# One tile of a 78-stage row sort is sorted by place and its four words are fetched through GpSimd

## The chip, the cores and the metric

The kernel runs on one core of one Trainium2 chip. Its time is device microseconds (us) for one execution, 17144.38 us in the median of three runs. VectorE is called DVE, ScalarE ACT, TensorE PE, GpSimd POOL and SyncE SP, as the profile does.

## What is computed

The input x is 32 images of 32 channels of 56x56 float32. Four layers follow each other, each as `x = x + layer(groupnorm(x))`. The last one holds nearly all the time:

```
xs = sort(x[:, :16], over rows), then sort over columns        # idx_h, idx_w kept
q  = conv1x1(x); qkv = fused 3x3/5x5/7x7 depthwise convs of q  # q1, k1, q2, k2, v
idx = argsort(v, over the 3136 pixels of a channel)
out1 = attention(q1[idx], k1[idx], v[idx]); out2 = attention(q2[idx], k2[idx], v[idx])
out = conv1x1(unsort(out1) * unsort(out2)); then both image sorts are undone on 16 channels
```

So each of the 1024 rows (batch, channel) of 3136 pixels is sorted by v, and four further words of each pixel (q1, k1, q2, k2) have to end in the same order.

## The kernel before

The rows lie as T = 8 tiles of 128 partitions; tile t holds batches 4t to 4t+3. All working buffers are slices of one SBUF tensor `arena`; `masks` holds four byte masks. Each engine has its own instruction list, and the work goes in rounds: at the end of a round every engine reports (`end_round`, L240) and SP opens the next one when all four have (`close_round`, L246). The rounds after the first layers:

- Four rounds **b** (`b_sync`, `b_scalar`, `b_vector`, L801 to L893) sort the images by rows and columns. U = 4 groups of eight batches, in the order 0, 1, 2, 3. From the second on, `c` of tile 0 runs beside them.
- **c** (`c_sync`, `c_tensor`, `c_scalar`, L923 to L975) makes the five words of one tile: SP loads 7 chunks of the padded image in 16 DMAs each (L930), PE makes 5 groups per chunk of 112 matmuls each (L951), so 35 groups, and ACT moves each from PSUM into `pay[b]` (four words, interleaved) or `vrow[b]` (L967). It makes a tile for the next round.
- Eight rounds **d** (`d_sync`, `d_scalar`, `d_vector`, L990 to L1098), here called d0 to d7, sort one tile each. The sorting network has 78 stages (`ROW_NET`). In a stage ACT first keeps the lower partners (of v at L1010, of the four words at L1020, in two lots). DVE compares v (L1046, a byte mask), takes minimum and maximum (L1054, L1061), and with the mask copies the upper partners down (L1070) and the kept ones up (L1077), each element four words wide. SP stores each mask to HBM (`row_masks`, L994), since the sort is undone later.
- **e** (`e_sync`, `e_scalar`, `e_vector`, `e_tensor`, L1146 to L1337) is the attention of a sorted tile. It ends with a store of the product (`prodd`, L1150).
- Two rounds **u** undo the row sort of four tiles each, with the masks loaded again; `u_first_sync` and `u_first_scalar` (L1437 to L1452) load and interleave the first four products. Two rounds **g** undo the image sorts.

What runs beside a sort is a Python generator: after each stage the sort calls `next(beside, None)` SLOTS = 4 times on SP, ACT and DVE, so a stage has four slots and a round 312. `c` evicts one group per four slots, the first after eight slots. `e` ends at slot 160 (E_LAST + 4). In round d(t), e of tile t-1 and c of tile t+1 run beside the sort:

```
d_sync(sp, 0, c_sync(sp, 1, CHUNKS, SLOTS))
...
d_sync(sp, i * 2 + k, chain(e_sync(sp, i * 2 + (k - 1)), c_sync(sp, i * 2 + (k + 1), CHUNKS, SLOTS)))
...
d_sync(sp, T - 1, chain(e_sync(sp, T - 2), u_first_sync(sp)))
u_sync(sp, 0, e_sync(sp, T - 1))
```

POOL has no work in the program: it takes part in the round ends only.

Of the kernel before, what the change touches and what calls it, by code (L numbers as in the profile page):

```python
# [16 lines left out]
N = H * W  # L17
P = 128
# [164 lines left out]
def program(nc, x, wdct_t, keep, ident_in, same_batch, same_head, shifts, sw, gate_w, temp,  # L183
# [4 lines left out]
    with ctx:  # L188
# [6 lines left out]
        rd = nc.dram_tensor("rd", (B * C, N), f32).ap()  # L195
        row_masks = nc.dram_tensor("row_masks", (T, P, ROW_PAIRS), u8).ap()
# [33 lines left out]
        sems = {}  # L230

        def sem(name):
            if name not in sems:
                sems[name] = ctx.enter_context(nc.semaphore(name))
            return sems[name]
# [10 lines left out]
        def close_round(sp, used):  # L246

            sp.wait_ge(round_done, len(go))
            for s in used:
                sp.sem_clear(s)  # L250
            sp.sem_clear(round_done)
            for n in go:
                sp.sem_inc(go[n], 1)  # L253
# [10 lines left out]
        s_const, s_rows, s_imgw, s_img, s_ydct = (sem(n) for n in (  # L264
            "s_const", "s_rows", "s_imgw", "s_img", "s_ydct"))
        s_chain, s_sq_in, s_sq_out = sem("s_chain"), sem("s_sq_in"), sem("s_sq_out")
        s_dct1, s_dct1c, s_dct2, s_dct2c = (sem(n) for n in ("s_dct1", "s_dct1c", "s_dct2", "s_dct2c"))
        s_taps, s_wmm, s_wcp = sem("s_taps"), sem("s_wmm"), sem("s_wcp")
        s_zero, s_norm = sem("s_zero"), sem("s_norm")
# [167 lines left out]
        a_x, a_y, a_st3, a_stp = sem("a_x"), sem("a_y"), sem("a_st3"), sem("a_stp")  # L437
        a_ch, a_sqi, a_sqo, a_norm = sem("a_ch"), sem("a_sqi"), sem("a_sqo"), sem("a_norm")
        a_sq, a_n2, a_n2e, a_nrm, a_nt = sem("a_sq"), sem("a_n2"), sem("a_n2e"), sem("a_nrm"), sem("a_nt")
        a_wide, a_rt, a_rni, a_sp = sem("a_wide"), sem("a_rt"), sem("a_rni"), sem("a_sp")  # L440
        a_g0, a_q, a_pr, a_dot, a_s, a_g, a_acc, a_half = (sem(n) for n in (
            "a_g0", "a_q", "a_pr", "a_dot", "a_s", "a_g", "a_acc", "a_half"))
        a_yv, a_yc, a_e, a_x3, a_xp = sem("a_yv"), sem("a_yc"), sem("a_e"), sem("a_x3"), sem("a_xp")
# [333 lines left out]

        b_in, b_out, b_mst = sem("b_in"), sem("b_out"), [sem(f"b_mst{i}") for i in range(4)]
# [17 lines left out]
        def b_begin(sp):  # L796

            b_load(sp, 0, bin_, b_in)
            b_load(sp, 0, bx, b_out)

        def b_sync(sp, u, beside, more=True):  # L801
            count = [0] * 4
            for d in range(2):
                for s, (at, _, n) in enumerate(IMG_NET):
# [8 lines left out]
                    if q == 5 and more:  # L813
                        sp.wait_ge(b_cp, 1)
                        sp.sem_clear(b_in)
                        b_load(sp, u + 1, bin_, b_in)
# [8 lines left out]
            if not more:  # L825
                sp.wait_ge(b_out, 16 * UB)
# [131 lines left out]
        def c_scalar(act, b, chunks, pace):  # L958

            n = 0  # L960
            for _ in range(2 * pace):
                yield
            for r in chunks:
# [138 lines left out]

        E_ROOT, E_RECIP, E_SCALE, E_TR, E_SEG, E_SEGS, E_OUT, E_NEXT = 8, 14, 16, 24, 8, 40, 76, 68
# [3 lines left out]
        e_sems = list(es.values())  # L1107
        st = [WS_AT]
# [37 lines left out]
        def e_sync(sp, t):  # L1146
            pace = Pace()
            yield from pace.to(E_LAST)
            sp.wait_ge(es["oc"], 16)
            sp.dma_start(prod_t[t], eo).then_inc(es["st"], 16)  # L1150
            sp.wait_ge(es["st"], 16)

        def e_scalar(act, b):
            e, pace = es, Pace()
# [78 lines left out]
        def e_vector(dve, b):  # L1233
            e, pace = es, Pace()
# [41 lines left out]
        def e_tensor(pe, b):  # L1276
            e = es
# [150 lines left out]
        prod_t4 = prodd.rearrange("(r w p) n -> r w p n", w=NP, p=P)  # L1428
        x3_t4 = x3d.rearrange("(r w p) n -> r w p n", w=NP, p=P)
        row_masks_t4 = row_masks.rearrange("(r w) p n -> r w p n", w=NP)  # L1430
        rd_t4 = rd.rearrange("(r w b c) n -> r w b c n", w=NP, b=TB, c=C)
        out_t4 = out.rearrange("(r w b c) n -> r w b c n", w=NP, b=TB, c=C)
# [4 lines left out]
        def u_first_sync(sp):  # L1437
# [3 lines left out]
            for w in range(NP):  # L1441
                if w >= 2:
                    yield from pace.to(8 + 12 * w)
                    sp.wait_ge(u_in, w - 1)
                sp.dma_start(uws[w % 2], prod_t4[0, w]).then_inc(u_ld[w], 16)
# [8 lines left out]
        def u_sync(sp, r, beside):  # L1454
            for i in range(SR):
# [3 lines left out]
                for w in range(NP):  # L1459
                    sp.dma_start(masks[:, w, 0:n], row_masks_t4[r, w, :, at:at + n]).then_inc(u_raw, 16)  # L1460
                for _ in range(SLOTS):
                    next(beside, None)
                if i == 60:
                    for _ in beside:
                        pass
                    for w in range(3):
                        sp.dma_start(u_x3[w], x3_t4[r, w]).then_inc(u_x[w], 16)
                    if r == 0:
                        for w in range(NP):
                            sp.dma_start(u_late[w], prod_t4[1, w]).then_inc(u_ld[w], 16)  # L1470
                    else:
                        g_load(sp, 0)
            for w in range(NP):
                sp.wait_ge(u_ev, 7 * (w + 1))
                for b in range(TB):
                    sp.dma_start(rd_t4[r, w, b, 0:CS], u_pr[w % 2][C * b:C * b + CS, :]).then_inc(u_rst[w % 2], 16)
                sp.wait_ge(u_add, 7 * (w + 1))
                for b in range(TB):
                    sp.dma_start(out_t4[r, w, b, CS:C], u_x3[w % 3][C * b + CS:C * b + C, :]).then_inc(u_ost, 16)
                if w == 0:  # L1480
                    sp.wait_ge(u_ost, 16 * TB)
                    sp.dma_start(u_x3[0], x3_t4[r, 3]).then_inc(u_x[0], 16)
# [170 lines left out]
        C_FIRST = [(0, 1, 2), (3, 4), (5, 6)]  # L1653

        @block.sync
        def _(sp):
# [15 lines left out]
            b_sync(sp, 0, iter(()))  # L1672
            close_round(sp, b_sems)
            for u in range(1, U):
                b_sync(sp, u, c_sync(sp, 0, C_FIRST[u - 1], 1), more=(u < U - 1))
                close_round(sp, b_sems + c_sems)
            d_sync(sp, 0, c_sync(sp, 1, CHUNKS, SLOTS))
            close_round(sp, d_sems + c_sems)
            with sp.Fori(0, (T - 2) // 2) as i:
                for k in (1, 2):  # L1680
                    d_sync(sp, i * 2 + k, chain(e_sync(sp, i * 2 + (k - 1)), c_sync(sp, i * 2 + (k + 1), CHUNKS, SLOTS)))
                    close_round(sp, d_sems + e_sems + c_sems)
            d_sync(sp, T - 1, chain(e_sync(sp, T - 2), u_first_sync(sp)))
            close_round(sp, d_sems + e_sems + u_first_sems)
            u_sync(sp, 0, e_sync(sp, T - 1))
# [11 lines left out]
        def _(pool):  # L1697
# [9 lines left out]
            with pool.Fori(0, U + T):  # L1707
                end_round(pool, "pool")
            end_round(pool, "pool")
# [5 lines left out]
        def _(act):  # L1715
# [14 lines left out]
            for u in range(1, U):  # L1730
                b_scalar(act, c_scalar(act, 0, C_FIRST[u - 1], 1))
                end_round(act, "act")
            d_scalar(act, 0, c_scalar(act, 1, CHUNKS, SLOTS))
            end_round(act, "act")
            with act.Fori(0, (T - 2) // 2):
                for k in (1, 0):
                    d_scalar(act, k, chain(e_scalar(act, 1 - k), c_scalar(act, 1 - k, CHUNKS, SLOTS)))
                    end_round(act, "act")
            d_scalar(act, 1, chain(e_scalar(act, 0), u_first_scalar(act)))
# [10 lines left out]
        def _(dve):  # L1750
# [18 lines left out]
            d_vector(dve, 0, iter(()))  # L1769
            end_round(dve, "dve")  # L1770
            with dve.Fori(0, (T - 2) // 2):
                for k in (1, 0):
                    d_vector(dve, k, e_vector(dve, 1 - k))
                    end_round(dve, "dve")
            d_vector(dve, 1, e_vector(dve, 0))
# [10 lines left out]
        def _(pe):  # L1786
# [14 lines left out]
            for u in range(1, U):  # L1801
                c_tensor(pe, C_FIRST[u - 1])
                end_round(pe, "pe")
            c_tensor(pe, CHUNKS)
            end_round(pe, "pe")
            with pe.Fori(0, (T - 2) // 2):
                for k in (1, 0):
                    e_tensor(pe, 1 - k)
                    c_tensor(pe, CHUNKS)
                    end_round(pe, "pe")  # L1810
            e_tensor(pe, 0)
            end_round(pe, "pe")
# [50 lines left out]
```

## Time and profile before

| | |
|---|---|
| median of 3 runs | 17144.38 us (17140.89 to 17151.51) |
| the profiled execution's own time | 17148.49 us |
| its span, first to last instruction | 17146.6 us |
| DVE busy | 16016.6 us, 93% of the span |
| ACT busy | 7247.1 us, 42% |
| PE busy | 6760.6 us, 39% |
| POOL busy | 0.2 us |
| DMA packets | 297993, 509.96 MB, 10% of 16 engines |

The profile is one execution; its time stands 4 us over the median. The trace behind it can be asked for any stretch: instructions in order of time, groups by line, the busy time of each engine per stretch, and the DMAs with the time from issue to landing. "Idle before" is the time an engine stood still before an instruction, with what ended it behind the arrow.

### The profile page before, as it was taken

Reading aid. Unit: us, or ns where it says so; the run is one execution under the profiler, and the core shown is the slowest. Engines: PE = TensorE matmul, PEld = TensorE weight load, DVE = VectorE, ACT = ScalarE, POOL = GpSimd, SP = SyncE. Lnnn points to the kernel's source line nnn. Section 1 sums busy time; section 2 is a strip of 40 time slices with the busy share of each in tenths; the row PEclk is TensorE's granted clock in tenths of the full one; section 3 lists DMA queues with packets and bytes.
Section 4 is the critical chain, followed back from the end, with each engine's and each line's share of the span. In section 5 each row is a group of like instructions: output and inputs, shape, how many; then the busy total and the mean of one; then the engine's idle time right before and its main releaser. Section 6 shows DMA issues by size and latency. Waiting matters only on the chain.

```text
span 17146.6 us, 106420 instructions
## 1 busy us (share of the span) xinstructions
PE 6760.6 (39%) x40644; PEld 2812.9 (16%) x40644; DVE 16016.6 (93%) x10433; ACT 7247.1 (42%) x5055; POOL 0.2 (0%) x4
## 2 busy tenths in 40 slices
PE   6888855570025614613722632642561101210010
PEld 4444431120011111201211211211111000000000
DVE  6999988899999999999999999999999998879978
ACT  0000003343453453444444444345345337868854
POOL 0000000000000000000000000000000000000000
PEclk9999987785567757856866866875775555555555
DMA  0000012110001000000100100100100001131232
GB/s 18 13 25 17 21 37 71 54 31 11 10 10 31 23 10 26 27 10 22 31 10 10 40 15 10 35 19 10 31 23 10 25 14 41 52 86 51 71 73 65
DMA packets 297993, 509.96 MB, mean 30 GB/s; under 512 B 54685, under 2 KB 258685, under 8 KB 287413
## 3 DMA queue, kind: packets, MB, share of 16 engines
q1 hardware_dynamic: 297460, 502.90, 10.3%
q8 instruction: 330, 5.41, 0.1%
q14 instruction: 203, 1.65, 0.0%
HBM read 298.39 MB, written 204.33 MB: 29 GB/s over the span
## 4 chain that ended last, share of the span: by engine, by line
DVE 60%; issue 10%; ACT 6%; PE 3%; DMA 1%; SPq 1%; DVEq 0%; ACTq 0%
DVE arena L1070 21%; DVE arena L1077 15%; DVE arena L1054 5%; DVE masks L1046 5%; DVE arena L1061 5%; DVE arena L1550 3%; PE psum L1332 2%; ACT arena L1497 2%; DVE arena L1548 2%; ACT arena L1020 2%; DVE arena L1401 1%; ACT arena L1507 1%; DMA masks<-row_masks 1%; ACT arena L1010 1%; DVE arena L1407 1%
## 5 line engine op out<-in xcount | busy, mean ns | idle before, releaser
L1020 ACT ACTIVATE arena<-arena 128x4096 f32<-128x4096 f32 (+26 forms) x1456 | 3072.3, 2127 | 5883.2 <-DVE arena L1077 5883.0
L951 PE MATMUL psum<-arena,wt 128*32 128x448 f32 x31360 | 3379.9, 594 | 1873.0 <-ACT arena L967 1126.7
L1070 DVE COPY_PREDICATED arena<-masks,arena 128x4096 f32<-128x4096 uint8 (+26 forms) x1456 | 4017.3, 2787 | 9.3 <-ACT arena L1020 9.3
L1077 DVE COPY_PREDICATED arena<-masks,arena 128x4096 f32<-128x4096 uint8 (+26 forms) x1456 | 4001.3, 2775 | 0.6
L951 PEld LDWEIGHTS psum<-arena,wt 128*32 128x32 f32 x31360 | 1047.2, 119 | 4208.2 <-issue 2660.3
L1287 PE MATMUL psum<-ident,arena 128*112 128x128 f32 x896 | 194.4, 386 | 3557.8 <-ACT arena L1208 2826.6
L1550 DVE COPY_PREDICATED arena<-arena 128x2048 f32<-128x2048 uint8 (+28 forms) x364 | 972.2, 2687 | 241.8 <-ACT arena L1507 241.6
L1046 DVE TENSOR_TENSOR masks<-arena 128x1568 uint8<-128x1568 f32 (+21 forms) x912 | 1033.9, 1192 | 128.9 <-ACT arena L1010 128.9
L731 PE MATMUL psum<-arena 128*128 128x392 f32 x3072 | 1053.8, 496 | 31.9 <-DVE arena L633 31.8
L1054 DVE TENSOR_TENSOR arena<-arena 128x1568 f32<-128x1568 f32 (+21 forms) x912 | 1056.3, 1220 | 0.0
L1061 DVE TENSOR_TENSOR arena<-arena 128x1568 f32<-128x1568 f32 (+21 forms) x912 | 1037.6, 1197 | 0.3
L1497 ACT ACTIVATE arena<-masks 128x4704 uint8<-128x4704 uint8 (+20 forms) x156 | 966.6, 6196 | 102.7 <-DMA masks<-row_masks 102.6
L1548 DVE COPY_PREDICATED arena<-arena 128x2048 f32<-128x2048 uint8 (+28 forms) x364 | 972.6, 2687 | 10.0
L1010 ACT ACTIVATE arena<-arena 128x1568 f32<-128x1568 f32 (+21 forms) x912 | 881.0, 997 | 79.0 <-SPq L253 68.3
L1507 ACT ACTIVATE arena<-arena 128x2048 f32<-128x2048 f32 (+28 forms) x364 | 762.9, 2120 | 276.2 <-DVE arena L1548 276.0
L1332 PE MATMUL psum<-arena 128*128 128x392 f32 x1024 | 583.6, 742 | 497.3 <-ACT arena L1178 378.8
L705 PE MATMUL psum<-arena 128*128 128x448 f32 (+1 forms) x1536 | 674.8, 589 | 252.0 <-DVE arena L621 220.3
L1323 PE MATMUL psum<-ident,arena 128*128 128x128 f32 x256 | 71.4, 434 | 1749.2 <-DVE arena L1266 1749.2
L1287 PEld LDWEIGHTS psum<-ident,arena 128*112 128x112 f32 x896 | 151.6, 197 | 3620.9 <-ACT arena L1208 2838.6
L1580 PE MATMUL psum<-arena,projm 128*128 128x448 f32 x112 | 88.8, 968 | 1596.5 <-DVE arena L1548 1596.5
L731 PEld LDWEIGHTS psum<-arena 128*128 128x128 f32 x3072 | 577.7, 191 | 481.9 <-DVE arena L633 86.5
L1302 PE MATMUL psum<-arena 112*128 112x512 f32 x896 | 486.9, 707 | 0.0
(126 smaller groups left out, 6794.2 us busy)
## 6 DMA issues: line engine op xcount, KB each, us to landing
arena<-xpad SPq DMA_DIRECT2D x896, 108.5 KB, 2.4
xpad<-arena SPq DMA_DIRECT2D x8, 1924.0 KB, 7.0
arena<-in_x SPq DMA_DIRECT2D x8, 1568.0 KB, 10.4
x3d<-arena SPq DMA_DIRECT2D x8, 1568.0 KB, 5.2
prodd<-arena SPq DMA_DIRECT2D x8, 1568.0 KB, 5.2
arena<-prodd SPq DMA_DIRECT2D x8, 1568.0 KB, 13.8
arena<-x3d SPq DMA_DIRECT2D x8, 1568.0 KB, 10.1
out<-arena SPq DMA_DIRECT2D x64, 196.0 KB, 4.5
```

The source lines that it names most:

```text
L731: last = nc.tensor.matmul(psum[:, i, 0:392], diag[:, kk, :], gg[2 * (g % 2) + n][:, 392 * i:392 * i + 392], start=False, stop=(g % NH == N ...
L951: last = nc.tensor.matmul(psum[C * b:C * b + C, n % C_BANKS, 0:CROWS * W], wt[:, g, C * w:C * w + C], cx[i % 2][b][:, y0:y0 + CROWS, x0:x0 ...
L1010: last = nc.scalar.activation(packed_view(vtmp, at, piece, 1), pair_views(vrow[b], piece, 1)[0], ACT.Copy)
L1020: last = nc.scalar.activation(packed_view(ptmp, here, piece, NP), pair_views(pay[b], piece, NP)[0], ACT.Copy)
L1046: last = nc.vector.tensor_tensor(packed_view(masks[:, q % 4, :], at, piece, 1), packed_view(vtmp, at, piece, 1), pair_views(vrow[b], piece ...
L1054: last = nc.vector.tensor_tensor(lo, packed_view(vtmp, at, piece, 1), hi, ALU.min)
L1061: last = nc.vector.tensor_tensor(hi, packed_view(vtmp, at, piece, 1), hi, ALU.max)
L1070: last = nc.vector.copy_predicated(lo, wide_mask(q, piece, at), hi)
L1077: last = nc.vector.copy_predicated(hi, wide_mask(q, piece, at), packed_view(ptmp, here, piece, NP))
L1497: nc.scalar.activation(um[i % 3][:, 0:NP * n].rearrange("p (n w) -> p w n", w=NP), masks[:, :, 0:n], ACT.Copy).then_inc(u_mk, 1)
L1548: last = nc.vector.copy_predicated(hi, mask, packed_view(utmp, here, piece, NP))
L1550: last = nc.vector.copy_predicated(lo, mask, hi)
```

## The change

Tile 7 is now the first one sorted, in a round of its own called **s**, and its four words are not moved by the network.

- The b rounds go in the order 3, 0, 1, 2, and c of tile 7 runs beside the last three.
- In round s, POOL writes into `spos` the number of each element (`128 rows x 3136`). The network moves v and this one position word: per stage DVE has compare, minimum, maximum and two single-word predicated copies, and ACT two keeps. SP first stores the four words of the tile to HBM (`payd`, 6.4 MB, 401,408 records of 16 bytes). c of tile 0 runs beside it.
- Then seven rounds d0 to d6 sort tiles 0 to 6 as before. POOL is not waited for at their ends (`LONG`). It stores the sorted places and v, and then in 64 chunks of 49 columns fetches the words: one indirect DMA per column, 128 records of 16 bytes each, 3136 in all; each chunk is stored to `payq`, and the places of the chunk after next are loaded.
- In round d6, after e of tile 5 (slot 160), SP waits for POOL (`p_done`), loads `payq` and v back, and e of tile 7 runs, then `u_first`. e of tile 6 runs in u0, as e of tile 7 did.

The core of the diff:

```diff
+        def s_sync(sp, t, beside):
+            sp.dma_start(payd.rearrange("(p n) w -> p (n w)", p=P), pay[0]).then_inc(s_pay, 16)
+            d_sync(sp, t, beside)
+            sp.wait_ge(s_pay, 16)
...
+        def s_scalar(act, beside):
+            def keep(q):
+                if q:
+                    act.wait_ge(d_vhi, q)
+                for piece, at in ROW_NET[q][1]:
+                    last = nc.scalar.activation(packed_view(vtmp, at, piece, 1), pair_views(vrow[0], piece, 1)[0],
+                                                ACT.Copy)
+                last.then_inc(d_vcp, 1)
+                if q:
+                    act.wait_ge(d_hi[0], q)
+                for piece, at in ROW_NET[q][1]:
+                    last = nc.scalar.activation(packed_view(stmp, at, piece, 1), pair_views(spos, piece, 1)[0],
+                                                ACT.Copy)
+                last.then_inc(d_cp[0], 1)
+            act.wait_ge(s_pos, 1)
+            keep(0)
+            for s in range(SR):
+                if s + 1 < SR:
+                    keep(s + 1)
+                for _ in range(SLOTS):
+                    next(beside, None)
...
+        def s_vector(dve):
+            dve.wait_ge(s_pos, 1)
...
+                for piece, at in rows:
+                    lo, hi = pair_views(spos, piece, 1)
+                    last = nc.vector.copy_predicated(lo, packed_view(masks[:, q % 4, :], at, piece, 1), hi)
...
+            dve.wait_ge(s_pay, 16)
+            dve.wait_ge(d_hi[0], SR)
+            nc.vector.tensor_copy(upos, spos)
...
+        def p_pool(pool):
+            pool.dma_start(posd, upos).then_inc(p_st, 16)
+            pool.dma_start(vsd, vrow[0]).then_inc(p_st, 16)
+            pool.wait_ge(p_st, 16 * 2)
+            for k in range(2):
+                pool.dma_start(gix[k], posd[:, GC * k:GC * k + GC]).then_inc(p_ix[k], 16)
+            def leave(c):
+                k = c % 2
+                pool.wait_ge(p_gat[k], 16 * GC * (c // 2 + 1))
+                at = GC * NP * c
+                pool.dma_start(payq[:, at:at + GC * NP], gout[k]).then_inc(p_out[k], 16)
+                if c + 2 < N // GC:
+                    at = GC * (c + 2)
+                    pool.dma_start(gix[k], posd[:, at:at + GC]).then_inc(p_ix[k], 16)
+            for c in range(N // GC):
+                k = c % 2
+                pool.wait_ge(p_ix[k], 16 * (c // 2 + 1))
+                if c >= 2:
+                    pool.wait_ge(p_out[k], 16 * (c // 2))
+                for j in range(GC):
+                    nc.gpsimd.indirect_dma_start(
+                        gout[k][:, NP * j:NP * j + NP], None, payd,
+                        bass.IndirectOffsetOnAxis(ap=gix[k][:, j:j + 1], axis=0)).then_inc(p_gat[k], 16)
+                if c:
+                    leave(c - 1)
...
+        def h_load_sync(sp):
+            sp.wait_ge(p_done, 1)
+            sp.dma_start(pay[0], payq).then_inc(h_ld, 16)
+            sp.dma_start(vrow[0], vsd).then_inc(h_ld, 16)
...
+        def h_load_scalar(act):
+            act.wait_ge(h_ld, 16 * 2)
...
-            d_sync(sp, 0, c_sync(sp, 1, CHUNKS, SLOTS))
-            close_round(sp, d_sems + c_sems)
...
-            d_sync(sp, T - 1, chain(e_sync(sp, T - 2), u_first_sync(sp)))
-            close_round(sp, d_sems + e_sems + u_first_sems)
-            u_sync(sp, 0, e_sync(sp, T - 1))
+            s_sync(sp, T - 1, c_sync(sp, 0, CHUNKS, SLOTS))
+            close_round(sp, d_sems + c_sems + [s_pos, s_pay])
             d_sync(sp, 0, c_sync(sp, 1, CHUNKS, SLOTS))
+            close_round(sp, d_sems + c_sems, LONG)
...
+            d_sync(sp, T - 2, chain(padded(e_sync(sp, T - 3), E_SLOTS), h_load_sync(sp),
+                                    padded(e_sync(sp, T - 1, hs), E_SLOTS), u_first_sync(sp)))
+            close_round(sp, d_sems + e_sems + h_sems + u_first_sems, LONG)
+            sp.sem_inc(go["pool"], 1)
+            u_sync(sp, 0, e_sync(sp, T - 2))
```

How the instructions stand, in the program's order.

SP at the start of the first sort round, before (`row_masks` are the mask stores, `arena<-xpad` the loads of c, 16 to a chunk):

```order
L820 DMA xpad<-arena 16x3848 x8
L250 ISA x12
L251 ISA
L994 DMA row_masks<-masks 128x1568 x2
L930 DMA arena<-xpad 32x868 x32
L994 DMA row_masks<-masks 128x784
```

and now:

```order
L826 DMA xpad<-arena 16x3848 x8
L255 ISA x12
L256 ISA
L1123 DMA payd<-arena 128x12544
L1002 DMA row_masks<-masks 128x1568 x2
L936 DMA arena<-xpad 32x868 x32
L1002 DMA row_masks<-masks 128x784
```

The 6.4 MB store of the words stands on the same queue ahead of the first loads of c.

SP in the last sort round, where `arena<-prodd` are the loads of `u_first`; before:

```order
L994 DMA row_masks<-masks 128x1456
L1150 DMA prodd<-arena 128x3136
L1445 DMA arena<-prodd 128x3136 x2
L994 DMA row_masks<-masks 128x1512
```

and now, at the same stage and at the end of the round:

```order
L1304 DMA prodd<-arena 128x3136
L1002 DMA row_masks<-masks 128x1512
L1288 DMA arena<-payq 128x12544
L1289 DMA arena<-vsd 128x3136
L1002 DMA row_masks<-masks 128x1540
...
L1002 DMA row_masks<-masks 128x1567
L1304 DMA prodd<-arena 128x3136
L1596 DMA arena<-prodd 128x3136 x4
```

The product loads of `u_first` moved from the middle of the round to behind its last mask store, and the loads of the fetched words took their place.

POOL behind round s (before, nothing but waits for the next round stands there):

```order
L1191 IOTA arena 128x3136
L249 ISA [waits go_pool]
L1196 DMA posd<-arena 128x3136
L1197 DMA vsd<-arena 128x3136
L1200 DMA arena<-posd 128x49 [waits p_st]
L1200 DMA arena<-posd 128x49
L1217 DMA arena<-payd,arena 128x4 [waits p_ix0]
L1217 DMA arena<-payd,arena 128x4 x48
L1217 DMA arena<-payd,arena 128x4 [waits p_ix1]
L1217 DMA arena<-payd,arena 128x4 x48
L1206 DMA payq<-arena 128x196 [waits p_gat0]
L1209 DMA arena<-posd 128x49
```

The list of places for a chunk is asked for only when the chunk two before has landed and the one before has been issued, and POOL waits for it at once.

## Rows read from the trace of the kernel before

**Rows 1.** The page: busy time of each engine, and the DMA queue.

```profile
PE 6760.6 (39%) x40644; PEld 2812.9 (16%) x40644; DVE 16016.6 (93%) x10433; ACT 7247.1 (42%) x5055; POOL 0.2 (0%) x4
q1 hardware_dynamic: 297460, 502.90, 10.3%
```

**Rows 2.** Windows, one per round (b, d0, d1, d7, u0): us, busy by engine, PEclk, DMA share, GB/s.

```profile
2880.00:3334.00 454.00, 223.72 (x2328) 69.97 (x2320) 369.88 (x346) 144.76 (x310) 0.00 (x0) 0.75 0.25 64
3334.00:4656.00 1322.00, 419.39 (x3920) 131.95 (x3920) 1308.09 (x706) 520.97 (x333) 0.00 (x0) 0.66 0.07 20
4656.00:6023.00 1367.00, 597.34 (x4304) 212.15 (x4304) 1338.86 (x774) 604.22 (x440) 0.00 (x0) 0.70 0.07 21
12843.00:14208.00 1365.00, 166.50 (x384) 80.24 (x384) 1336.87 (x781) 600.61 (x410) 0.00 (x0) 0.55 0.04 16
14208.00:15410.00 1202.00, 209.76 (x440) 91.49 (x440) 1010.97 (x462) 953.20 (x396) 0.00 (x0) 0.57 0.22 62
```

**Rows 3.** DVE in order of time: first instruction of d0, d1, d7 and u0.

```profile
3334.79 1.79 DVE L1046 TENSOR_TENSOR masks<-arena 128x1568 uint8<-128x1568 f32 x1 [20.97 <-ACT arena L1010]
4657.10 1.79 DVE L1046 TENSOR_TENSOR masks<-arena 128x1568 uint8<-128x1568 f32 x1 [4.39 <-ACT arena L1010]
12870.96 1.79 DVE L1046 TENSOR_TENSOR masks<-arena 128x1568 uint8<-128x1568 f32 x1 [4.08 <-ACT arena L1010]
14230.78 4.68 DVE L1550 COPY_PREDICATED arena<-arena 128x4220 f32<-128x4220 uint8 x1 [17.96 <-ACT arena L1507]
```

**Rows 4.** Groups by line within d0.

```profile
L1070 DVE COPY_PREDICATED arena<-masks,arena 128x2048 f32<-128x2048 uint8 (+24 forms) x182 | 499.6, 2771 | 1.1 <-ACT arena L1020 1.1
L1077 DVE COPY_PREDICATED arena<-masks,arena 128x2048 f32<-128x2048 uint8 (+24 forms) x182 | 497.5, 2758 | 0.1
L1054 DVE TENSOR_TENSOR arena<-arena 128x64 f32<-128x64 f32 (+31 forms) x114 | 132.8, 1214 | 0.0
L1061 DVE TENSOR_TENSOR arena<-arena 128x64 f32<-128x64 f32 (+31 forms) x114 | 129.6, 1186 | 0.0
L1046 DVE TENSOR_TENSOR masks<-arena 128x64 uint8<-128x64 f32 (+31 forms) x114 | 129.2, 1182 | 29.5 <-ACT arena L1010 29.5
L1010 ACT ACTIVATE arena<-arena 128x64 f32<-128x64 f32 (+31 forms) x115 | 112.9, 1012 | 15.4 <-SPq L253 13.3 <-DVE arena L1061 2.0
```

**Rows 5.** Groups by form: one-word predicated copy (in g), and DVE's longest of L1077.

```profile
L1401 DVE COPY_PREDICATED arena<-masks,arena 128x1568 f32<-128x1568 uint8 x16 | 29.3, 1884 | 2.6 <-ACT arena L1389 2.6
L1054 DVE TENSOR_TENSOR arena<-arena 128x1568 f32<-128x1568 f32 x6 | 10.8, 1796 | 0.0
L1077 DVE COPY_PREDICATED arena<-masks,arena 128x4088 f32<-128x4088 uint8 x16 | 77.8, 4864 | 0.0
```

**Rows 6.** PE in order of time: ten groups of c in a b round, the first in d0.

```profile
2935.80 108.02 PE L951 MATMUL psum<-arena,wt 128*32 128x448 f32 x1120 [47.83 <-DMA arena<-xpad]
3356.72 43.60 PE L951 MATMUL psum<-arena,wt 128*32 128x448 f32 x440 [100.97 <-DMA arena<-xpad]
```

**Rows 7.** DMA issues: line engine op xcount, KB each, median us from issue to landing.

```profile
arena<-xpad SPq DMA_DIRECT2D x896, 108.5 KB, 2.4
prodd<-arena SPq DMA_DIRECT2D x8, 1568.0 KB, 5.2
arena<-prodd SPq DMA_DIRECT2D x8, 1568.0 KB, 13.8
row_masks<-masks SPq DMA_DIRECT2D x32, 96.0 KB, 1.7
```

**Rows 8.** SP's issues of c's loads (L930), minimum, median, maximum in ns.

```profile
L930 SPq DMA_DIRECT2D arena<-xpad x848: 310/316/2053, 2925.6 to 12626.4; - x170
```

**Rows 9.** Groups by line within d7: minimum of v, and the copies of u_first.

```profile
L1054 DVE TENSOR_TENSOR arena<-arena 128x64 f32<-128x64 f32 (+31 forms) x114 | 124.6, 1119 | 0.0
L1452 ACT ACTIVATE arena<-arena 128x3136 f32<-128x3136 f32 x4 | 23.5, 5872 | 0.0
```

More of the change, by code:

```diff
@@ L812, in b_sync @@
                         next(beside, None)
[L813 removed]
+                    if q == 5 and more is not None:
                         sp.wait_ge(b_cp, 1)
                         sp.sem_clear(b_in)
[L816 removed]
+                        b_load(sp, more, bin_, b_in)
             sp.wait_ge(b_xp, 1)
@@ L824, in b_sync @@
                 sp.wait_ge(b_mst[i], 16 * count[i])
-            if not more:
+            if more is None:
                 sp.wait_ge(b_out, 16 * UB)
@@ L956, in c_tensor, with c_scalar @@
                     n += 1
-        def c_scalar(act, b, chunks, pace):
+        def c_scalar(act, b, chunks, pace, free=None):
             n = 0
@@ L962, in c_scalar @@
                 yield
+            if free is not None:
+                act.wait_ge(free, 16 * 2)
             for r in chunks:
@@ L1100, in d_vector @@
                 pass
+        s_pos, s_pay = sem("s_pos"), sem("s_pay")
+        p_st, p_ix, p_gat, p_out, p_done = (sem("p_st"), [sem(f"p_ix{k}") for k in range(2)], [sem(f"p_gat{k}") for k in range(2)],
+                                            [sem(f"p_out{k}") for k in range(2)], sem("p_done"))
+        GC = 49
+        spos = ptmp[:, 0:N]
+        stmp = ptmp[:, N:N + TMP]
+        upos = pay[0][:, 0:N].bitcast(mybir.dt.uint32)
+        st = [WS_AT + 8448]
+        gix = [take(st, GC).bitcast(mybir.dt.uint32) for _ in range(2)]
@@ new lines, in program @@
+        gout = [take(st, GC * NP) for _ in range(2)]
+        def s_sync(sp, t, beside):
[23 more added lines that the diff above has]
+                    next(beside, None)
+            for _ in beside:
+                pass
@@ new lines, in s_pool @@
+        def s_pool(pool):
+            nc.gpsimd.iota(spos, pattern=[[1, N]], base=0, channel_multiplier=N,
+                           allow_small_or_imprecise_dtypes=True).then_inc(s_pos, 1)
+        def p_pool(pool):
[23 more added lines that the diff above has]
+                    leave(c - 1)
+            leave(N // GC - 1)
+            for k in range(2):
+                pool.wait_ge(p_out[k], 16 * (N // GC // 2))
+            pool.dma_reset()
+            for x in (*p_ix, *p_gat, *p_out):
+                pool.sem_clear(x)
+            pool.sem_inc(p_done, 1)
@@ L1801, in _ @@
             for u in range(1, U):
-                c_tensor(pe, C_FIRST[u - 1])
+                c_tensor(pe, C_FIRST[u])
                 end_round(pe, "pe")
[L1804 to L1807, printed above, removed]
+            for _ in range(2):
+                c_tensor(pe, CHUNKS)
+                end_round(pe, "pe")
+            with pe.Fori(0, (T - 4) // 2):
+                for k in (0, 1):
                     e_tensor(pe, 1 - k)
```

189 lines of the change are left out of this document (128 added, 61 removed).

## Prediction

> **What bounds the kernel now.** I read the page first: DVE is busy for 93% of the span, POOL not at all [rows 1]. The windows per round then show where: in d0, DVE is busy 1308 of 1322 us and PE only 419; d1 and d7 are as full, and only the b, u and g rounds leave DVE gaps [rows 2]. The starts of the rounds give their lengths: d0 lasts 1322.3 us, d1 to d6 last (12870.96 - 4657.10) / 6 = 1369.0 us each, d7 1359.8 us with its 18 us of idle at the end [rows 3]. So e, which is in d1 and not in d0, costs 46.7 us of round, and c nothing. Groups by line in d0: the two four-word predicated copies take 997.1 us of a sum of 1388.7, the three operations on v 391.6 [rows 4]. DVE is the bound of every sort round, and what a round costs is what its list holds. The sum of the durations exceeds the busy time by 81 us over 706 instructions, so neighbours overlap by 0.114 us.
>
> **Round s.** It replaces one d round.
>
> DVE: the v operations stay, 391.6 us [rows 4]. A position copy has one word. No sort round shows such a copy; the rounds that undo the image sorts do: 1.884 us for 1568 elements where minimum takes 1.796 [rows 5], 5% more. With 114 pieces as for v that is 2 x 131 x 1.05 = 275 us. Sum 667 us, less 570 x 0.114 = 65: **602 us**.
>
> ACT: two keeps of 113 us and 35 evictions of 1 us, no bound in themselves. The keep of v runs while DVE copies positions, the keep of positions while DVE compares.
>
> PE: here is the new bound. c makes 35 groups and ACT takes one per stage, the first in stage 2, the last in stage 36. A mean d stage lasts 17 us, longer than a group; a stage of s would last 602 / 78 = 7.7 us. Uninterrupted, PE makes ten groups in 108.0 us, 10.8 each [rows 6]. ACT stands in its list before the eviction, and behind it are the keeps that DVE needs, so the first 37 stages go at PE's pace. In d0 PE starts 22 us after the first compare [rows 3, 6]. Now the 6.4 MB of words lie ahead on SP's queue; 1.6 MB take 5.2 us to landing [rows 7], so 21 us, of which some 13 pass before the loads of c are issued: start at 30 us. The last group is there at 30 + 35 x 10.8 = 408 us. From stage 38 on the network has 55,822 of its 104,995 pairs, 53%, so 320 us of DVE. With one eviction, the cast of positions, POOL's counting pattern at the start and 4.4 us of round change [rows 3] I take **S = 745 us**; 630 if PE did not hold it back, 1123 if PE ran at 1.2 GHz, at double the time per group.
>
> Saved: 1322 - 745 = 577 us. The e's and c's in the other sort rounds are as many as before (seven e's in d1 to d7, now five in d1 to d5 and two in d6).
>
> **Round d6.** Two e's need 320 slots and a round has 312. So e of tile 7 is stored after the last stage and the whole of `u_first` follows behind it, where before it was hidden in d7. Store 5.2 us; the first load some 8 [rows 7]; then four copies of 5.9 us [rows 9], the last two waiting for loads that can only start when a buffer comes free, 33 us in all: **+38 us**. Bounds: 24 us (the copies alone) to 66 (store, four loads of 13.8 one after another and a copy).
>
> The load of the fetched words, 7.8 MB: 26 us by the 5.2 us row. SP issues it at the compare of stage 41, ACT comes to its wait some 16 us later and DVE has one more stage of 17 us: **+4 us**, 0 to 40.
>
> **Rounds d0 to d6 with POOL at work.** POOL has run nothing beside DVE, so this is unknown. The fetch writes 6.4 MB in 16-byte pieces. c's loads, 12 MB a round, go with a minimum operation of 132.8 us in d0 against 124.6 in d7 [rows 4, 9]; on the sum of DVE that is some 50 us per 12 MB, so **+25 us** for the fetch, by bytes. Lower bound 0. Upper bound: each of the 3136 gathers breaks one overlap of DVE and adds as much again, 2 x 0.114 = 0.23 us: 715 us. I take the bytes, since the rows show that form of disturbance and no other.
>
> **Does the fetch fit?** POOL may begin when s closes, and its result is needed in d6 at stage 41, after 51% of the pairs: 1322 + 5 x 1369 + 0.506 x 1322 + 47 = 8883 us. It needs 3136 gathers, 128 other DMAs, and 64 times the landing of a place list (2.4 us [rows 7]), plus 13 us at the start. With g the time of one, 3264 g + 167 us must stay below 8883: **g below 2.67 us**. Bounds of g: 0.32 us, what SP takes to issue a DMA [rows 8], and 2.4 + 4.9 = 7.3 us, a full landing and the longest DVE instruction [rows 5, 7]. A store of a mask is the nearest, 128 rows in one DMA: 1.7 us from issue to landing [rows 7]. I take that, which gives 5.7 ms, ended in d4. The DMA engines: 297,460 packets took 10.3% of 16 engines, 95 ns each [rows 1]; 401,408 more are 2.4 ms spread over those rounds, and mask stores have three stages of slack.
>
> **Sum** against the profiled execution: 17148.5 - 577 + 38 + 4 + 25 = 16,639; its time stands 4 us over the median, so 17,144 - 510 = **16,634 us**.
>
> **Rivals.**
>
> *1. POOL is too slow.* A gather on POOL has to wait for the DVE instruction that runs, and DVE never pauses in these rounds [rows 2]. With mean instructions of 1.97 us and long ones of 4.8 an arrival waits about 1.5 us: g = 3.2, the fetch takes 10.6 ms, SP stands at stage 41 for 1.7 ms, mask stores and DVE behind it: 16,634 + 1730 = 18,360 us. It decides from 2.67 us on, and breaks even with the time before at 2.83; at 3.06 it is 17,900. For it: DVE's fullness. Against: nothing shows that the two share anything.
> The Trainium skill, page "SBUF — State Buffer", section "Who interferes with whom", has a rule that speaks for it: a DVE instruction with two SBUF inputs (all of these have) and a GpSimd instruction that reads SBUF exclude each other, and the second waits for the whole of the first. The same page has a GpSimd DMA at 620 ns alone and 3100 ns beside a DVE copy; by that figure the fetch would take 10.3 ms and the kernel 18,036 us. No row here shows POOL beside DVE.
>
> *2. POOL fits but holds DVE up.* The same exclusion the other way round: each gather delays DVE by d. The gain of 535 us before any disturbance is spent at d = 0.17 us. At 0.1 us the time is 16,609 + 314 = 16,923; at 0.2 us 17,236, slower.
>
> *3. The saving is not there.* PE at 1.2 GHz in s: S = 30 + 35 x 21.6 + 320 + 17 = 1123, 378 more, 17,012 us. Against it: PE will be busier than in the b rounds, where ten groups took 108 us [rows 6].
>
> **How the numbers follow.** My forecast, with its own range 16,580 to 16,760, has 46%. Rival 2 with a gain 13%, with about no change 4%, with a loss 8%. Rival 1 has 26%: 10 of them below 17,900, 1 of these within 0.2%. Rival 3 has 3%. A measurement of this kernel can tell 0.2%, 34 us, from no change. So faster 0.62, same 0.05, slower 0.33. The range goes from 16,580 to 17,900; above are 16%, below 2%.
>
> **What would show it.** Round s at 745 us with ACT waiting for PE in its first 37 stages and DVE at some 90% in the others; DVE groups of the d rounds within 2% of [rows 4]; POOL's gathers 1.7 us apart and ended two rounds before d6; some 56 us of DVE idle between d6 and u0 against 18. An SP wait at stage 41 of d6 would make the prediction wrong by its length; predicted copies of over 2.85 us in the d rounds that shrink when POOL ends would show rival 2.

## The result, and the profile after

The kernel became slower: **19,204.75 us** in the median of four runs (19,193.31 to 19,213.78), against 17,144.25 us for the kernel before beside them. The ratio is 1.1201, with a 95% interval from 1.1181 to 1.122. I had forecast 16,634 us, with a range up to 17,900.

The page of the changed kernel: busy time, the DMA queues, the chain that ended last by engine, the group of the indirect transfers, and their time to landing.

```profile
PE 6695.3 (35%) x40644; PEld 2794.7 (15%) x40644; DVE 15423.9 (80%) x10298; ACT 6997.9 (36%) x4986; POOL 10391.5 (54%) x3271
...
q1 hardware_dynamic: 297892, 517.35, 9.4%
q0 software_dynamic: 105760, 17.87, 1.7%
...
POOL 54%; DVE 10%; issue 9%; ACT 4%; PE 3%; DMA 2%; SPq 0%; DVEq 0%; POOLq 0%; ACTq 0%
...
L1217 POOL DMA_INDIRECT arena<-payd,arena x3136 | 10312.4, 3288 | 1049.2 <-issue 936.9
...
arena<-payd,arena POOLq DMA_INDIRECT x3136, 2.4
```

DVE fell from 16,016.6 us [rows 1] to 15,423.9, as the change intends. POOL rose from nothing to 10,391.5, and over half of the chain now runs through its gathers (L1217). One took 3.29 us in the mean, and 0.30 us lie between two.

The waits name the place where this comes due. Columns: us in total, times, longest.

```profile
ACT arena L1345 <- DMA arena<-vsd: 2604.9, 1, 2604.9
```

DVE's first instruction behind it:

```profile
15578.14 4.57 DVE L1078 COPY_PREDICATED arena<-masks,arena 128x4032 f32<-128x4032 uint8 x1 [2598.28 <-ACT arena L1028]
```

From 12,979.9 us, stage 41 of d6, DVE stands still for 2598.3 us, because ACT waits for the fetched words. Windows: round s in two pieces, d0, d1, d6 up to the stall, the stall, the rest of d6 (columns as in [rows 2]).

```profile
3340.00:3740.00 400.00, 370.83 (x3920) 116.23 (x3920) 362.72 (x242) 156.88 (x133) 0.00 (x0) 0.96 0.19 59
3740.00:4097.00 357.00, 0.00 (x0) 0.00 (x0) 351.60 (x330) 115.04 (x131) 0.41 (x1) 0.50 0.06 20
4097.00:5417.00 1320.00, 419.36 (x3920) 134.33 (x3920) 1305.82 (x706) 520.32 (x333) 1280.37 (x103) 0.66 0.08 23
5417.00:6784.00 1367.00, 596.46 (x4304) 212.44 (x4304) 1338.94 (x774) 604.50 (x440) 1310.74 (x173) 0.70 0.08 21
12260.00:12979.00 719.00, 164.35 (x384) 79.00 (x384) 704.72 (x427) 341.12 (x259) 675.18 (x139) 0.59 0.05 13
12980.00:15578.00 2598.00, 0.00 (x0) 0.00 (x0) 0.00 (x0) 10.07 (x9) 1906.32 (x2044) 0.50 0.08 7
15578.00:16240.00 662.00, 164.65 (x384) 79.16 (x384) 643.36 (x413) 307.67 (x244) 0.00 (x0) 0.60 0.03 10
```

POOL is "busy" for 1280 of 1320 us in d0 and ends 103 instructions in it. In the stall, with DVE idle, it ends 2044. Of the 3136 gathers, 1175 began before the stall, in 8.87 ms, and 1961 in its 2598 us. The sum closes: +2598.3 from the stall, -542.1 from all the rest, +2056.2 us between the spans 17,146.6 and 19,202.8.

What a gather does beside DVE is seen in order of time (start, duration). In the first 25 us of d0:

```profile
4121.33 4.74 DVE L1078 COPY_PREDICATED arena<-masks,arena 128x4096 f32<-128x4096 uint8 x1
4122.54 4.32 POOL L1217 DMA_INDIRECT arena<-payd,arena  x1 [0.30 <-issue]
4125.97 2.25 DVE L1054 TENSOR_TENSOR masks<-arena 128x784 uint8<-128x784 f32 x1
4127.16 1.89 POOL L1217 DMA_INDIRECT arena<-payd,arena  x1 [0.30 <-issue]
4128.14 4.89 DVE L1085 COPY_PREDICATED arena<-masks,arena 128x4096 f32<-128x4096 uint8 x1
4129.36 4.47 POOL L1217 DMA_INDIRECT arena<-payd,arena  x1 [0.31 <-issue]
4132.92 2.73 DVE L1078 COPY_PREDICATED arena<-masks,arena 128x2176 f32<-128x2176 uint8 x1
```

The gather of 4122.54 waits for the copy that ends at 4126.07 and ends 0.79 us behind it; those of 4127.16 and 4129.36 end 0.83 and 0.80 us behind the DVE instruction they waited for. That is rival 1 as written. But 50 us later the pattern is another:

```profile
4181.17 1019.06 POOL L1217 DMA_INDIRECT arena<-payd,arena  x1 [0.30 <-issue]
...
5198.13 1.27 DVE L1069 TENSOR_TENSOR arena<-arena 128x1088 f32<-128x1088 f32 x1
...
5200.53 0.94 POOL L1217 DMA_INDIRECT arena<-payd,arena  x1 [0.30 <-issue]
5200.55 2.79 DVE L1078 COPY_PREDICATED arena<-masks,arena 128x2048 f32<-128x2048 uint8 x2 [1.15 <-ACT arena L1028]
```

One gather waits **1019 us**, over 572 DVE instructions, and ends when DVE itself stood still for 1.15 us. Before the stall 37 of the 1175 gathers waited longer than 30 us, 4750 us in all. Inside such a wait, here one that began at 7474.49 and took 278.88 us, DVE's neighbours overlap:

```profile
7600.59 2.43 DVE L1078 COPY_PREDICATED arena<-masks,arena 128x1536 f32<-128x1536 uint8 x1
7602.45 2.02 DVE L1062 TENSOR_TENSOR arena<-arena 128x1344 f32<-128x1344 f32 x1
7603.91 2.41 DVE L1085 COPY_PREDICATED arena<-masks,arena 128x1536 f32<-128x1536 uint8 x1
```

7600.59 + 2.43 is 0.57 us behind the next start. All pairs of neighbours on DVE that both read two inputs in SBUF, up to the stall and while a gather waited, were counted by whether it got in there. Its entry is taken as 0.91 us before its end, and it belongs to a pair if it lies between 0.25 us before the first one's end and the start of the second:

```
the next instruction starts       pairs   the gather gets in
after the end (a real gap)           82     82
up to 0.125 us before it           2287    816   (36%)
earlier still                      1972     22   ( 1%)
```

Where the 37 long waits ended is less one-sided. 13 ended at a real gap (5 of these inside e), 16 between a two-input instruction and one of e that reads one input or PSUM, and 8 between overlapping two-input neighbours. One that ended in front of an instruction of e:

```profile
5448.63 36.10 POOL L1217 DMA_INDIRECT arena<-payd,arena  x1 [0.30 <-issue]
5481.38 2.53 DVE L1078 COPY_PREDICATED arena<-masks,arena 128x2176 f32<-128x2176 uint8 x1
5483.80 0.17 DVE L1400 TENSOR_SCALAR small<-small 128x8 f32<-128x8 f32 x1
```

The theory for the experiments was this: **a GpSimd instruction that reads SBUF gets in only where DVE's stream of two-input instructions has a gap, and a stream that overlaps closes the door for any length of time.** Rivals: the writing of descriptors or the queue limits the gathers (B); or the gaps that count are those of the one-input and PSUM instructions of e, for which those 21 of the 37 ends speak.

### The profile page after: what moved, and what is told of

Its sections match the earlier page's. It is cut to its first block, busy times and chain, and to the rows that moved or that the text cites. A ratio compares the mean times of both kernels' runs of the same rounds, so it can differ in the third digit from the quotient of the medians.

```text
span 19202.8 us, 108759 instructions
## 1 busy us (share of the span) xinstructions
PE 6695.3 (35%) x40644; PEld 2794.7 (15%) x40644; DVE 15423.9 (80%) x10298; ACT 6997.9 (36%) x4986; POOL 10391.5 (54%) x3271
## 4 chain that ended last, share of the span: by engine, by line
POOL 54%; DVE 10%; issue 9%; ACT 4%; PE 3%; DMA 2%; SPq 0%; DVEq 0%; POOLq 0%; ACTq 0%
POOL arena L1217 54%; DVE arena L1701 3%; PE psum L957 2%; ACT arena L1648 2%; DVE arena L1699 2%; DVE arena L1078 1%; DVE arena L1554 1%; ACT arena L1658 1%; DVE arena L1085 1%; DMA arena<-posd 1%; DMA masks<-row_masks 1%; DVE arena L1560 1%; PE psum L1485 1%; DVE arena L1178 0%; PE psum L1731 0%
## 5 line engine op out<-in xcount | busy, mean ns | idle before, releaser
L1217 POOL DMA_INDIRECT arena<-payd,arena x3136 | 10312.4, 3288 | 1049.2 <-issue 936.9
L1078 DVE COPY_PREDICATED arena<-masks,arena 128x2048 f32<-128x2048 uint8 (+22 forms) x1274 | 3523.2, 2797 | 2606.4 <-ACT arena L1028 2606.4
L1028 ACT ACTIVATE arena<-arena 128x2048 f32<-128x2048 f32 (+22 forms) x1274 | 2688.0, 2127 | 5103.5 <-DVE arena L1085 5103.5
L957 PE MATMUL psum<-arena,wt 128*32 128x448 f32 x31360 | 3319.9, 586 | 2060.3 <-DMA arena<-xpad 1103.1
L1085 DVE COPY_PREDICATED arena<-masks,arena 128x2048 f32<-128x2048 uint8 (+22 forms) x1274 | 3506.5, 2783 | 0.4
L1345 ACT ACTIVATE arena<-arena 128x784 f32<-128x784 f32 x128 | 203.1, 1587 | 2607.9 <-DMA arena<-vsd 2604.9
L1054 DVE TENSOR_TENSOR masks<-arena 128x64 uint8<-128x64 f32 (+34 forms) x798 | 909.1, 1202 | 89.1 <-ACT arena L1018 89.1
L1062 DVE TENSOR_TENSOR arena<-arena 128x64 f32<-128x64 f32 (+34 forms) x798 | 928.4, 1229 | 0.0
L1069 DVE TENSOR_TENSOR arena<-arena 128x64 f32<-128x64 f32 (+34 forms) x798 | 911.1, 1204 | 0.2
L1018 ACT ACTIVATE arena<-arena 128x64 f32<-128x64 f32 (+34 forms) x798 | 771.0, 997 | 77.5 <-SPq L258 67.8
```

Of the source, the lines that this page charges most:

```text
L957: last = nc.tensor.matmul(psum[C * b:C * b + C, n % C_BANKS, 0:CROWS * W], wt[:, g, C * w:C * w + C], cx[i % 2][b][:, y0:y0 + CROWS, x0:x0 ...
L1028: last = nc.scalar.activation(packed_view(ptmp, here, piece, NP), pair_views(pay[b], piece, NP)[0], ACT.Copy)
L1062: last = nc.vector.tensor_tensor(lo, packed_view(vtmp, at, piece, 1), hi, ALU.min)
L1069: last = nc.vector.tensor_tensor(hi, packed_view(vtmp, at, piece, 1), hi, ALU.max)
L1078: last = nc.vector.copy_predicated(lo, wide_mask(q, piece, at), hi)
L1085: last = nc.vector.copy_predicated(hi, wide_mask(q, piece, at), packed_view(ptmp, here, piece, NP))
```

## The experiments

Each is an edit of the changed kernel. The kernel before ran beside them on the same chip, at 17,145 to 17,152 us in the median.

**plain.** The transfers stay, with their shape, count and order, but take no place list. This leaves out the fetch by place: the words of tile 7 come back unsorted.

```diff
-                    nc.gpsimd.indirect_dma_start(
-                        gout[k][:, NP * j:NP * j + NP], None, payd,
-                        bass.IndirectOffsetOnAxis(ap=gix[k][:, j:j + 1], axis=0)).then_inc(p_gat[k], 16)
+                    at = NP * (GC * c + j)
+                    pool.dma_start(gout[k][:, NP * j:NP * j + NP], pay_rows[:, at:at + NP]).then_inc(p_gat[k], 16)
```

> The 3136 indirect DMAs are replaced by as many plain DMAs from GpSimd of the same shape, 128 records of 16 bytes each, from fixed places. This leaves out the fetch by place: the words of tile 7 keep their unsorted order. Theory A (an indirect DMA has to read its list of places from SBUF, and DVE's instructions with two SBUF inputs keep it from that): a plain DMA reads no list, so each takes 0.6 us as the 64 plain stores did, plus 0.3 us between them, the fetch ends 2.9 ms after round s, nothing waits at stage 41 of d6, and the time is 19204.75 - 2598 = 16607 us. Theory B (writing descriptors, or the DMA rings and the traffic of c, hold GpSimd up): the plain DMAs wait as the indirect ones did, and the time stays near 19200 us. This run also gives what the rest of the change is worth.

Measured: 16,611.72 us, ratio 0.969 [0.9673, 0.9706].

```profile
L1220 POOL DMA_DIRECT2D arena<-payd x3136 | 1687.1, 547 | 133.3 <-DMA arena<-posd 123.6 <-issue 3.4
```

0.547 us each (0.667 at most), no stall. The number of POOL's transfers and their bytes cost nothing that these runs can tell (`fill`, below, fetches nothing and takes 16,613.02 us), and the rest of the change is worth 533 us. What lengthens the gathers is bound to their being fetched by a place list.

**breath1 and breath7.** A memset of one column on DVE, once or seven times in a stage of the d rounds, to open a place between two-input instructions. breath7 puts this call behind each of the seven groups of a stage, breath1 only behind the last:

```diff
+            def breath():
+                turn[0] += 1
+                c = 52 + turn[0] % 12
+                nc.vector.memset(small[:, c:c + 1], 0.0)
```

> The change, with one memset of 128x1 at the end of each stage on DVE in d0 to d6 (an instruction without an SBUF input, 546 in all). Theory A: each lets the waiting gather in. The 37 waits of over 30 us, 4750 us in all, are broken up into stages of 17 us; at the 3.6 us per gather seen outside them, 1300 more gathers get through before stage 41 of d6, 660 are left at 1.25 us, and the time is 16607 + 825 + 50 = 17480 us. Theory B: the memsets open nothing, 19200 us.

> The same with seven memsets per stage, one behind each group of DVE instructions (3780 in all, one per 2.5 us). Theory A: a gather gets in behind each group, 2.5 us apart, so all 3136 are through in 7.9 ms, before stage 41 of d6; no wait there. The memsets cost 0.1 us each, 380 us, and the time is 16607 + 380 = 16990 us, just faster than before. Theory B: 19200 us + 380.

Measured: 18,807.34 us for breath1, ratio 1.0992 [1.0944, 1.1039], and 17,979.0 for breath7, 1.0501 [1.0472, 1.0529]. Both missed, by 1330 and 990 us; the direction was right, the size was not. Waits of hundreds of us remained (breath7, in order of time):

```profile
7599.45 357.11 POOL L1231 DMA_INDIRECT arena<-payd,arena  x1 [0.30 <-issue]
7648.83 4.75 DVE L1085 COPY_PREDICATED arena<-masks,arena 128x3840 f32<-128x3840 uint8 x1
7653.24 1.94 DVE L1061 TENSOR_TENSOR masks<-arena 128x1488 uint8<-128x1488 f32 x1
7653.52 0.06 DVE L1054 MEMSET small<- 128x1 f32 x1
7654.86 0.40 DVE L1061 TENSOR_TENSOR masks<-arena 128x16 uint8<-128x16 f32 x1
```

The memset takes 0.06 us and lies at 7653.52, while the copy of 7648.83 still runs (to 7653.58) and the comparison of 7653.24 has begun. It makes no gap. The seven together cost 61 us of time (17,898.7 - 1229.4 of stall - 16,608.6), 0.016 us each.

Still the memsets let more gathers through: 1599 began before the stall in breath1 and 2280 in breath7, against 1175. At the end of a stage, where breath1 has its memset, a waiting gather got in at 202 of 460 overlapping neighbours, against 105 of 462 in the changed kernel, and real gaps were no more frequent. How the memset does it is not shown. And a wide overlap is not needed to keep a gather out. In breath1 one waited 840.6 us,

```profile
4237.79 840.56 POOL L1225 DMA_INDIRECT arena<-payd,arena  x1 [0.30 <-issue]
```

while 468 of the 478 pairs of neighbours overlapped by 0.125 us or less.

**pause1 and pause4.** So DVE was made to stop for a moment: it waits for the semaphore that its own last instruction sets. pause1 has only the last of these lines, pause4 all four.

```diff
                 lower(s, 0)
+                dve.wait_ge(d_lo[0], s + 1)
...
                 upper(s, 0)
+                dve.wait_ge(d_hi[0], s + 1)
...
                 lower(s, 1)
+                dve.wait_ge(d_lo[1], s + 1)
...
                 upper(s, 1)
+                dve.wait_ge(d_hi[1], s + 1)
```

> Once in each of the 78 stages of the seven payload sorts VectorE waits for the end of its own last instruction before it issues the next one, so that nothing runs on it for a moment, where the memset of breath1 ran inside the overlap of its neighbours. Theory (a waiting gather gets in where VectorE's neighbours leave a real gap, 80 of 80 times in the trace of the changed kernel, and seldom where they overlap by over 0.12 us): no wait is longer than about two stages (35 us), so the fetch has some 1,500 gathers done before the load of the fetched words is waited for in stage 41 of d6, against 1,175 in the changed kernel; the rest run at 1.25 us each in the stall, (3136 - 1500) x 1.25 = 2,045 us. The pauses cost some 0.2 us each, 546 x 0.2 = 110 us. Time 16,607 + 110 + 2,045 = about 18,760 us, and no wait of a gather over 100 us. Rival (the gap is not what counts; gathers get in beside the one-input and PSUM instructions of the e step, which this edit does not touch): 19,203 + 110 = about 19,310 us, with waits of several hundred us as before.

> The same pause behind each of the four payload exchanges of a stage, 2,184 in all. Theory: one gather gets in at each pause and some of the others at the chance gaps, some 2,400 before stage 41 of d6, so the stall is (3136 - 2400) x 1.25 = 920 us; the pauses cost some 0.2 us each, 440 us. Time 16,607 + 440 + 920 = about 17,970 us, the longest wait below 20 us. Rival (the gap is not what counts): 19,203 + 440 = about 19,640 us, with the long waits as before.

Measured: pause1 17,508.27 us, ratio 1.0212 [1.0189, 1.0235]; **pause4 16,926.69 us**, ratio 0.9868 [0.9852, 0.9885], faster than the kernel before. Both are far faster than either theory said. As the only way in, the instructions of e fall as a rival (19,310 and 19,640 us); my theory holds in kind, and forecast too small an effect. What the pauses do, on the tile of the gathers: count, then minimum, median and maximum in ns, first and last start.

```profile
L1221 POOL DMA_INDIRECT arena<-payd,arena x3136: 940/1930/6431, 4112.5 to 12429.5; - x196
```

No gather of pause4 waits over 6.4 us. The last one starts at 12,429.5, in d6 but ahead of stage 41, so there is no stall. In pause1 the longest before the stall is 18.7 us, about one stage, and the stall is

```profile
DVE arena L1078 <- ACT arena L1028: 796.4, 8, 789.3
```

where the changed kernel had 2598.3 us. Where a gather waited, counted as above, it got in at all 532 real gaps of pause1 and at all 1556 of pause4. But in pause4 it also got in at 1771 of 1871 two-input neighbours that overlapped by up to 0.125 us, 95% where the changed kernel had 36%. So the pauses do more than open their own gaps, and what more is not shown. The price of a pause is (16,931.7 - 16,608.6) / 2184 = 0.148 us and, in pause1, (17,474.2 - 789.3 - 16,608.6) / 546 = 0.140.

**pause2 and pause3.** With this price the number of pauses could be fitted to the deadline: pause2 has those behind the two `upper`, pause3 also the one behind `lower(s, 1)`, and in d6 none past stage 41.

```diff
-        def d_vector(dve, b, beside):
+        def d_vector(dve, b, beside, gaps=SR):
...
+                if s < gaps:
+                    dve.wait_ge(d_lo[1], s + 1)
...
-            d_vector(dve, 1, chain(padded(e_vector(dve, 0), E_SLOTS), e_vector(dve, 0, hs)))
+            d_vector(dve, 1, chain(padded(e_vector(dve, 0), E_SLOTS), e_vector(dve, 0, hs)), 41)
```

> The pause behind two of the four payload exchanges of a stage (the two upper ones), 1,092 in all. pause1 had 3136 - 789/1.25 = 2,505 gathers done before stage 41 of d6, and pause4 all of them 550 us before it. Theory (each gap admits one gather, pauses cost 0.148 us as the 2,184 of pause4 did with 323 us): about 2,950 done by then, a stall of some 230 us, pauses 162 us: 16,609 + 162 + 230 = about 17,000 us, between 16,770 (no stall) and 17,200. Rival (one pause a stage already does what pauses can, and the second adds nothing): 17,508 + 80 = 17,590 us.

> The pause behind three of the four exchanges, and in d6 only up to stage 41, where the fetched words are waited for: 3 x (6 x 78 + 41) = 1,527 pauses. Theory: the fetch ends shortly before stage 41 of d6, no stall, 16,609 + 1,527 x 0.148 = about 16,835 us, the fastest of all kernels here. Rival (the fetch falls short by some hundred gathers): up to 200 us more, 17,035 us.

Measured: 17,030.77 us for pause2, ratio 0.9935 [0.9918, 0.9951], with ACT waiting 254.2 us for the fetched words; **16,834.91 us for pause3**, ratio 0.9817 [0.9801, 0.9834]. Both came out within 31 us of the forecast. The gathers of pause3:

```profile
L1223 POOL DMA_INDIRECT arena<-payd,arena x3136: 941/1897/11563, 4107.7 to 12960.4; - x196
```

The last gather starts 206 us before SP comes to the load of the fetched words:

```profile
13166.02 0.43 SPq L1294 DMA_DIRECT2D arena<-payq  x1
```

So not all of its 1527 pauses were needed; the 12,979.9 us of the changed kernel is no deadline here, since the pauses themselves move stage 41 back. pause3 is the best kernel of this study, 315 us (1.8%) faster than the one before.

**copy and fill.** Is it the gather, or any work of POOL? Each transfer becomes a GpSimd instruction on the same four columns; the fetch is left out in both.

```diff
# copy
+                    nc.gpsimd.tensor_copy(gout[k][:, NP * j:NP * j + NP],
+                                          gix[k][:, j:j + 1].bitcast(f32).to_broadcast([P, NP])).then_inc(p_gat[k], 16)
# fill
+                    nc.gpsimd.memset(gout[k][:, NP * j:NP * j + NP], 1.0).then_inc(p_gat[k], 16)
```

> Each indirect transfer becomes a GpSimd copy of its index to the four columns (SBUF to SBUF, 128x4), so nothing is fetched by place. Theory A (what waits is any GpSimd instruction that reads SBUF, while VectorE's two-input instructions overlap): copies wait as the gathers did, hundreds of us at a time, and there is a stall at stage 41 of d6; a copy is shorter than a gather, some 0.2 us, so that the rest of them costs less there: 1,961 x 0.2 = some 400 us or less, 16,610 + 400 = about 17,000 us. Theory B (only the writing of an indirect transfer's descriptors waits so): copies of some 0.2 us each, no wait over 10 us, 16,610 us.

> Each indirect transfer becomes a GpSimd memset of its four columns, which writes SBUF and reads nothing; nothing is fetched by place. Theory A1 (it is the read of SBUF that waits): fills of some 0.1 to 0.2 us each, no long wait, 16,610 us. Theory A2 (any access of GpSimd to SBUF waits): as the copies, waits of hundreds of us and some 17,000 us.

Measured: copy 16,618.89 us, ratio 0.9691 [0.9675, 0.9707]; fill 16,613.02, 0.9688 [0.9672, 0.9704]. The copies, by source line (columns as above):

```profile
L1217 POOL COPY arena<-arena x3136: 177/185/1086886, 4111.8 to 12802.2; 128x4 f32<-128x4 f32 x196
```

as a group of the page:

```profile
L1217 POOL COPY arena<-arena 128x4 f32<-128x4 f32 x3136 | 8521.0, 2778 | 107.0 <-DMA arena<-posd 107.0
```

and the fills, by source line:

```profile
L1217 POOL MEMSET arena<- x3136: 97/98/108, 4108.7 to 4413.3; 128x4 f32 x196
```

This is the cleanest pair. A copy that takes 0.185 us in the median waited up to **1086.9 us**, and all copies 8.5 ms; an instruction that only writes SBUF never waited, 0.108 us at most. The fills were all done in the first 305 us of d0, a stretch in which only 3 copies, or 14 gathers of the changed kernel, could begin. So for a GpSimd instruction it is the read of SBUF (theory B falls a second time). That a gather waits for the same reason, to read its place list, is the reading that fits `plain`, `copy` and `fill` together; no run gives a gather its list in another way. My time for copy was wrong, 17,000 against 16,619: being short, several copies pass in one opening, and the last began at 12,802.2, before stage 41.

## Why the prediction was wrong

- **The failed step: "A store of a mask is the nearest ... 1.7 us from issue to landing. I take that", for g.** A gather costs POOL 1.25 us with DVE idle (0.947 and 0.30 between two; 1961 in 2598 us is 1.32 with the chunk changes). So 1.7 was a fair price for the gather alone. Beside DVE it took 8.87 ms / 1175 = 7.5 us: the sum had no term for POOL's wait at DVE, and with it "Does the fetch fit?" comes out the other way. The row I took from, a transfer that SP issues without reading anything in SBUF itself, is like `plain` (0.547 us), not like a gather.
- **Rival 1 was right in kind and too mild in size.** It has "an arrival waits about 1.5 us: g = 3.2" and 18,360 us. A gather that waits for one instruction exists (rows at 4122 us), and where nearly all are like it, there is no stall: pause4 is that case, at 2.65 us per gather (4112.5 to 12,429.5, 3136 of them), just within the threshold of 2.67. In the changed kernel most of the waiting passes over hundreds of instructions. My upper bound, 7.3 us from a full landing and the longest DVE instruction, was beaten even by the mean, 7.5. The Trainium skill, page "SBUF — State Buffer", section "Who interferes with whom", has the exclusion between a DVE instruction with two SBUF inputs and a GpSimd instruction that reads SBUF, the second waiting for the whole of the first. `copy` and `fill` agree with who excludes whom. They do not agree with one instruction as the length of the wait. Its 3100 ns for a GpSimd DMA beside DVE gave 18,036 us; the mean over the run here, 3288 ns, is near it only because nearly two thirds of the gathers ran in the stall.
- **The threshold was right, and so was the place.** "An SP wait at stage 41 of d6 would make the prediction wrong by its length": 16,634 + 2598 = 19,232, against 19,205.
- **Round s**: 757.4 us against 745, by another division. The position copies took 172.9 + 172.3 = 345 us, not 275: the 5% over a minimum that [rows 5] show for 1568 elements is 33% in the mean of all forms, 1.56 us against 1.17. And PE held DVE back less than I said: at a granted clock of 0.96, 35 groups in 400 us, DVE was idle for 37 us of them, where 408 us were to cover half a network of 602. The two errors cancel.
- **Rival 2**, DVE held up by the gathers, is refuted: d0 lasts 1320.2 us against 1322.3, and d1 to d5 1368.4 in the mean against 1369.0. Only the durations in the records grow, by 2% (next fence); their overlap grows with them. So the +25 us for contention is 0 (its "some 50 us per 12 MB" came from one operation, 132.8 us against 124.6, that was carried over to all of DVE), and without it the sum of the rest is -535 where `plain` shows -533.

```profile
L1078 DVE COPY_PREDICATED arena<-masks,arena 128x2048 f32<-128x2048 uint8 (+24 forms) x182 | 510.0, 2848 | 1.1 <-ACT arena L1028 1.1
L1085 DVE COPY_PREDICATED arena<-masks,arena 128x2048 f32<-128x2048 uint8 (+24 forms) x182 | 507.8, 2834 | 0.1
```

These answer to the first two of [rows 4], 499.6 and 497.5.

- **The tail of d6**: DVE is idle for 55.6 us before u0, as forecast (56):

```profile
16296.52 4.68 DVE L1701 COPY_PREDICATED arena<-arena 128x4220 f32<-128x4220 uint8 x1 [55.60 <-ACT arena L1658]
```

- **Rival 3** did not come: PE ran at 0.96 of full speed in s, so near its upper level.

The chance of 0.26 for rival 1 was too low for another reason: I wrote "nothing shows that the two share anything" against it. The profile of before has POOL at 0.2 us, so it could not have shown it. Silence of a trace in which one partner does not run says nothing about the two together.

## What to carry to other kernels

Before work is handed to GpSimd beside a full DVE, ask whether it reads SBUF. In this kernel, where it only wrote there or issued plain transfers, it ran freely; where it read, its price was set not by its own length but by how often DVE's stream let it in, which real stops always did. Where it must read, give DVE a short stop on purpose, here a wait for its own last instruction at 0.148 us, and place only as many as the deadline needs. Here 1527 stops, still some more than that, cost 226 us and turned a loss of 2060 us into a gain of 315.

## What the runs showed of the hardware that I had not expected

- A 128x4 GpSimd copy of 0.185 us waited up to 1086.9 us behind DVE instructions with two SBUF inputs, and an indirect DMA up to 1019 us. A GpSimd memset (0.098 us) and plain DMAs issued from GpSimd (0.547 us) were never held up.
- The exclusion is one-sided: DVE's rounds lost nothing, even with POOL "busy" for 97% of d0. Where a profile shows a busy POOL, that can be waiting alone.
- A DVE memset of one column runs inside the overlap of its neighbours, 0.016 us of time each, and makes no gap, yet 3801 of them shortened the stall from 2598 to 1229 us; a wait on DVE's own last semaphore costs 0.14 to 0.15 us, and a waiting gather got in at every real gap counted.
- Left open: why some overlapping neighbours let a gather in and others do not. The width of the overlap is no account of it: up to 0.125 us let in 36% in the changed kernel and 95% in pause4, and at 468 such pairs within one wait of breath1 nothing. Overlaps of 0.25 us and more are 7 of 706 pairs in d0 of the kernel before and 341 of 705 in the changed kernel, but also 106 of 704 in fill, where nothing waited, and none of 705 in breath1 (its memsets left out), where gathers did. So they are neither the cause nor a sure mark of a waiting gather. The pauses show that a gap lets it in; they do not show what keeps it out.
